# A transformer block on one core: the second MLP product as three passes over rounded parts, the keys' parts made in SBUF

## The reference, cut to what matters

```python
x_norm = modulate(_ln(x), shift_a, scale_a)
q, k, v = jnp.split(x_norm @ W_qkv + b_qkv, 3, axis=-1)
...                                   # softmax attention, W_proj, gate_a, residual
q_c = _ln(x) @ W_qc + b_qc
k_c, v_c = jnp.split(_ln(context) @ W_kvc + b_kvc, 2, axis=-1)
...                                   # softmax attention, W_cproj, residual
x_norm2 = modulate(_ln(x), shift_m, scale_m)
h = jax.nn.gelu(x_norm2 @ W_mlp1 + b_mlp1)
h = h @ W_mlp2 + b_mlp2               # the second MLP product
x = x + gate_m[:, None] * h
```

## Time and profile before

| | |
|---|---|
| median of 3 runs | 854.02 us (851.39 to 857.76) |
| profiled execution | 854.26 us, its span 852.4 us |
| PE busy | 814.3 us (96%) |
| DVE busy | 626.7 us (74%) |
| ACT busy | 489.6 us (57%) |
| POOL busy | 395.0 us (46%) |
| mean granted clock | 0.970 of full speed |

### The profile page before, as it was taken

How to read it: one execution, slowest core, us unless ns; L and a number is a source line. 1 busy time by engine, 2 the same in 40 slices (tenths; PEclk the granted TensorE clock), 3 DMA queues, 4 the chain that set the end, 5 groups by cost and what they waited for, 6 DMA issues and landing times.

```text
span 852.4 us, 19187 instructions
## 1 busy us (share of the span) xinstructions
PE 814.3 (96%) x6968; PEld 615.5 (72%) x6968; DVE 626.7 (74%) x1368; ACT 489.6 (57%) x923; POOL 395.0 (46%) x451
## 2 busy tenths in 40 slices
PE   6797989999999999999999999999999999998997
PEld 4666667778777777778787777777777778675776
DVE  5758897787868687887868787887868687764421
ACT  2153656657565656657575656657575656675242
POOL 3365446355454636365463637365463635251301
PEclk9698899999999999999999999999999999999899
DMA  7534453433434333433344343334334333211001
GB/s 261 163 115 137 143 157 114 110 114 111 129 114 134 108 122 118 126 96 119 120 114 137 105 129 117 119 95 126 112 114 142 100 104 107 65 39 62 26 1 38
DMA packets 92903, 95.05 MB, mean 112 GB/s; under 512 B 17993, under 2 KB 79562, under 8 KB 92426
## 3 DMA queue, kind: packets, MB, share of 16 engines
q1 hardware_dynamic: 91946, 92.77, 35.1%
q10 hardware_dynamic: 864, 1.07, 0.4%
HBM read 38.55 MB, written 4.32 MB: 50 GB/s over the span
## 4 chain that ended last, share of the span: by engine, by line
PE 88%; DVE 5%; POOL 2%; issue 2%; DMA 1%; ACT 1%; SPq 1%; DVEq 0%; ACTq 0%; POOLq 0%
PE bank L830 23%; PE scan L932 15%; PE pv L877 14%; PE bank L864 13%; PE bank L855 7%; PE bank L844 6%; PE score L942 5%; PE bank L804 2%; DVE MX_x L1297 1%; DMA P<-in_wm 1%; DVE MX_y L1297 1%; DVE W L1307 0%; ACT P L1092 0%; PE score L781 0%; DVE PT L1204 0%
## 5 line engine op out<-in xcount | busy, mean ns | idle before, releaser
L1092 ACT ACTIVATE P<-score 128x512 f32<-128x512 f32 x512 | 283.3, 598 | 217.9 <-PE score L942 215.9
L1297 DVE TENSOR_REDUCE MX_x<-scan 128x2 fp32r<-128x512 f32 x256 | 170.0, 678 | 66.5 <-PE scan L932 66.2
L1297 DVE TENSOR_REDUCE MX_y<-scan 128x2 fp32r<-128x512 f32 x256 | 165.3, 677 | 30.3 <-PE scan L932 28.9
L830 PE MATMUL bank<-xT_y,W 128*128 128x256 f32 x960 | 131.0, 293 | 5.2 <-DVE xT_y L1172 2.6
L830 PEld LDWEIGHTS bank<-xT_y,W 128*128 128x128 f32 x960 | 122.8, 198 | 10.8 <-issue 7.2
L864 PE MATMUL bank<-w_down,HH 128*128 128x256 f32 x512 | 125.6, 390 | 0.0
L932 PE MATMUL scan<-KS_x,QS_x 63*128 63x256 f32 x512 | 109.5, 324 | 8.4 <-DVE MX_x L1297 7.6
L932 PEld LDWEIGHTS scan<-KS_x,QS_x 63*128 63x128 f32 x512 | 72.4, 191 | 47.8 <-issue 22.8
L942 PE MATMUL score<-QS_y,KS_y 64*128 64x256 f32 x512 | 104.1, 318 | 1.4 <-ACT P L1092 1.4
L864 PEld LDWEIGHTS bank<-w_down,HH 128*128 128x128 f32 x512 | 93.0, 191 | 16.7 <-issue 0.6
L932 PEld LDWEIGHTS scan<-KS_y,QS_y 63*128 63x128 f32 x512 | 69.0, 190 | 48.9 <-DVE MX_y L1297 23.6
(11 more groups left out here) (139 smaller groups left out, 1272.2 us busy)
## 6 DMA issues: line engine op xcount, KB each, us to landing
KS_x<-SK SPq DMA_DIRECT2D x96, 128.0 KB, 2.1
KS_y<-SK SPq DMA_DIRECT2D x96, 128.0 KB, 2.1
...
```

Source lines behind the costliest of these rows:

```text
L830: last = nc.tensor.matmul(to[:, i * N:(i + 1) * N], w[p][:, c, (blk + i) * 128:(blk + i + 1) * 128], xT[k][:, q, c, :], start=(n == 0), st ...
L1092: nc.scalar.activation(P[:, s % 8, :, :].rearrange("p a n -> p (a n)"), score_bank[s % 2][:, :], ACT.Exp, scale=SCALE).then_inc(s_exp, 1)
L1297: nc.vector.tensor_reduce(MX[s1][:, half, col:col + NB], scan_bank[n % NSCAN][:, :].rearrange("p (a n) -> p a n", a=NB), AXIS.X, ALU.max, ...
```

## The change

1. **Second MLP product.** `w_down` becomes a part of `W`, split by a new task `w6` (HI on ACT, LO on DVE, 2048 columns each) in section B of t = 1, from `raw_down`, which now lies where LO will be. The gelu output goes to `hidden`, which lies over the LO half of a doubled `HH`; a new POOL task `h0` to `h3` casts 128x512 into HI and subtracts into LO (`rest`); for the last element DVE does that (`hidden_parts`). A half of `down` is now 4 x 3 = 12 `f32r` matmuls.
2. **Keys.** ACT writes `keys` (over the LO half of `SK`) from PSUM and then copies it to HI; POOL makes LO by a subtraction (`keys_rest`). The bank is free once `keys` is written. DVE's two instructions per key task go.
3. **Scratch** for dynamic transfers is set to 512 bytes, which makes room for the larger `HH` and `W`.
4. **The tables** are written anew for the steady sections; those of the first and last turns keep their order but for the added tasks.

```diff
-        w_down = sb("w_down", [128, FB, H])
+        w_down = weight(5120, FB, H)
...
+        keys = over("keys", [128, 2, N], sk_at + 4 * 2 * N)
...
+        HH, hh_at = placed("HH", [128, 2, FB, N], f32r)
+        hidden = over("hidden", [128, FB, N], hh_at + 4 * FB * N)
...
+            def keys_rest(name, b):
+                if name == "k_x" and b == 0:
+                    return
+                pool.wait_ge(s_hi[name], nth(name, b))
+                nc.gpsimd.tensor_tensor(SK[:, LO, :, :], keys[:, :, :], SK[:, HI, :, :].bitcast(fp32),
+                                        ALU.subtract).then_inc(s_lo[name], 1)
+
+            def rest(u, b):
+                if b == B - 1:
+                    return
+                pool.wait_ge(s_gelu[u], b + 1)
+                at = slice(2 * u, 2 * u + 2)
+                nc.gpsimd.tensor_copy(HH[:, HI, at, :], hidden[:, at, :]).then_inc(s_HH[u], 1)
+                pool.wait_ge(s_HH[u], 2 * b + 1)
+                nc.gpsimd.tensor_tensor(HH[:, LO, at, :], hidden[:, at, :], HH[:, HI, at, :].bitcast(fp32),
+                                        ALU.subtract).then_inc(s_HH[u], 1)
...
             def down(a, b, part, to):
                 if b == 0:
-                    pe.wait_ge(s_wdown, 16)
-                pe.wait_ge(s_HH, FB // 2 * b + FB // 4 * (part + 1))
+                    pe.wait_ge(s_wlo[6], 1)
+                for u in (2 * part, 2 * part + 1):
+                    pe.wait_ge(s_HH[u], 2 * b + 2)
                 for c in range(part * FB // 2, (part + 1) * FB // 2):
-                    last = nc.tensor.matmul(to[:, 0:H], HH[:, c, a * 128:(a + 1) * 128], w_down[:, c, :],
-                                            start=(c == 0), stop=(c == FB - 1))
+                    for n, (p, q) in enumerate(PARTS):
+                        last = nc.tensor.matmul(to[:, 0:H], HH[:, p, c, a * 128:(a + 1) * 128], w_down[q][:, c, :],
+                                                start=(c == 0 and n == 0), stop=(c == FB - 1 and n == 2))
...
                 for i in range(2):
-                    last = nc.scalar.activation(dst[:, HI, i, :], src[:, i * N:(i + 1) * N], ACT.Identity,
+                    to = keys[:, i, :] if name in ("k_x", "k_y") else dst[:, HI, i, :]
+                    last = nc.scalar.activation(to, src[:, i * N:(i + 1) * N], ACT.Identity,
                                                 bias=bias_cols[:, col + i:col + i + 1])
+                if name in ("k_x", "k_y"):
+                    last.then_inc(s_keys[name], 1)
+                    act.wait_ge(s_keys[name], nth(name, b))
+                    last = nc.scalar.activation(SK[:, HI, :, :].rearrange("p c n -> p (c n)"),
+                                                keys[:, :, :].rearrange("p c n -> p (c n)"), ACT.Copy)
...
+    "B1": [("q_x", 1, 4), ("q_x", -1, 6), ("k_y", 0, 15), ("w6", -1, 15)],
```

More of the change, by code:

```diff
@@ L28 @@
 SP_PLAN = {
[L29 to L32 removed]
+    "A": [("gate_a", 0, 0), ("xT_in", 2, 0), ("x_in", 2, 0), ("max_x0", 0, 1), ("st_c", 0, 3), ("q_y0", -1, 3),
+          ("mr_c", 0, 3), ("q_y1", -1, 6), ("k_x", 1, 7), ("max_x1", 0, 7), ("c_in", 1, 8), ("q_x", 1, 9), ("st_x",
+          2, 9), ("max_y0", -1, 10), ("mr_x", 2, 11), ("k_y", 0, 12), ("gate_m", -2, 14), ("cT_in", 1, 15)],
     "A-1": [("c_in", 1, 7), ("cT_in", 1, 12)],
@@ L93 @@
 ACT_PLAN = {
-    "A": [("v_x", 0, 1), ("up0", -3, 3), ("up1", -3, 3), ("T_x", 1, 3), ("up2", -3, 3), ("up3", -3, 3), ("T_y", -1,
-          8), ("k_x", 1, 8), ("q_y", -1, 10), ("q_x", 1, 13)],
+    "A": [("v_x", 0, 1), ("T_x", 1, 2), ("up0", -3, 3), ("up1", -3, 3), ("up2", -3, 3), ("up3", -3, 3), ("T_y", -1,
+          8), ("k_x", 1, 8), ("q_y", -1, 10), ("q_x", 1, 12)],
     "A-1": [],
@@ L106 @@
     "AB+2": [],
-    "B": [("v_y", -1, 3), ("k_y", 0, 9), ("T_m", -2, 11)],
+    "B": [("v_y", -1, 4), ("k_y", 0, 9), ("T_m", -2, 11)],
     "B0": [("q_x", 1, 8)],
-    "B1": [("q_x", 1, 4), ("q_x", -1, 6), ("k_y", 0, 15)],
+    "B1": [("q_x", 1, 4), ("q_x", -1, 6), ("k_y", 0, 15), ("w6", -1, 15)],
     "BB-1": [("T_m", -2, 12)],
@@ L237, in dram, with placed, over @@
             return nc.dram_tensor(name, shape, dt, kind="Internal").ap()
-        W = sb("W", [128, 2, 5120], f32r)
+        def placed(name, shape, dt):
+            at = (nc.sbuf_base + 31) // 32 * 32
+            return sb(name, shape, dt), at
+        def over(name, shape, at):
+            return nc.alloc_sbuf_tensor_at(name, shape, fp32, offset=at)
+        W, w_at = placed("W", [128, 2, 7168], f32r)
         def weight(start, blocks, cols):
@@ L307, in build @@
         raw_kvc = [to[:, :, :].rearrange("p a c -> p (a c)") for to in (x2, x2_bias)]
-        raw_up = HH[:, :, :].rearrange("p a b -> p (a b)")
-        rows = HH[0:B, 0:5, :]
+        raw_up, raw_down = [over(n, [128, 2048], w_at + 4 * (7168 + start))[:, :]
+                            for n, start in (("raw_up", 3072), ("raw_down", 5120))]
+        rows = hidden[0:B, 0:5, :]
         d_gate = dram("d_gate", (B, 4 * H))
@@ L355, in build @@
         s_centred = {k: sem(f"s_centred_{k}") for k in "xc"}
+        s_keys = {k: sem(f"s_keys_{k}") for k in ("k_x", "k_y")}
         s_hi = {k: sem(f"s_hi_{k}") for k in ("T_y", "q_x", "k_x", "q_y", "k_y")}
@@ L362, in build @@
         s_MT = {s: [sem(f"s_MT_{s}{i}") for i in range(2)] for s in "xy"}
-        s_HH = sem("s_HH")
+        s_gelu, s_HH = [[sem(f"{n}{u}") for u in range(4)] for n in ("s_gelu", "s_HH")]
         s_scan_full, s_scan_done = sem("s_scan_full"), sem("s_scan_done")
@@ L573, in load_down @@
             def load_down(b):
-                sp.dma_start(w_down[:, :, :], wdown).then_inc(s_wdown, 16)
+                sp.dma_start(raw_down, wdown).then_inc(s_raw[6], 16)
             def last_row_x0(b):
@@ L751, in _ @@
                 "sum0": lambda b: total(0, b), "sum1": lambda b: total(1, b),
+                **{f"h{u}": lambda b, u=u: rest(u, b) for u in range(4)},
+                **{k: lambda b, k=k: keys_rest(k, b) for k in ("k_x", "k_y")},
                 **{f"clear{i}": lambda b, i=i: clear(i) for i in range(5)}, "clear_V": clear_values,
@@ L979, in copied @@
             def copied(name, k, b):
-                wait(act, s_HH, FB // 2 * (b - 1))
+                for u in range(4):
+                    wait(act, s_gelu[u], b - 1)
                 src = full(act, name, b)
@@ L1078, in _ @@
                 "v_y": lambda b: values("y", b),
-                **{f"w{i}": lambda b, i=i: split_weight(i) for i in range(1, 6)},
+                **{f"w{i}": lambda b, i=i: split_weight(i) for i in range(1, 7)},
             }
@@ L1187, in projected @@
             def projected(name, dst, col, b):
-                if b == 0 and name in ("q_x", "k_x"):
-                    if name == "k_x":
-                        first_projected()
+                if b == 0 and name == "q_x":
                     return
@@ L1274, in _ @@
                 "q_y": lambda b: projected("q_y", SQ["y"], QYC, b),
-                "k_y": lambda b: projected("k_y", SK, KYC, b),
                 "q_x": lambda b: projected("q_x", SQ["x"], QXC, b),
-                "k_x": lambda b: projected("k_x", SK, KXC, b),
+                "k_x": first_projected,
+                **{f"h{u}": lambda b, u=u: hidden_parts(u, b) for u in range(4)},
                 "down0": lambda b: down(0, b),
                 "down1": lambda b: down(1, b),
-                **{f"w{i}": lambda b, i=i: split_weight(i) for i in range(1, 6)},
+                **{f"w{i}": lambda b, i=i: split_weight(i) for i in range(1, 7)},
                 "norm_x": norm_early, "T_x": lambda b: split_end("x", b),
```

101 lines of the change are left out of this document (58 added, 43 removed), and 29 rows, old and new, of tables (DVE_PLAN, PE_PLAN, POOL_PLAN).

## The result

| | before | after |
|---|---|---|
| median of 19 runs | 853.15 us (850.42 to 857.76) | 857.29 us (851.92 to 863.58) |
| ratio | | 1.0043, 95% interval 1.0025 to 1.0061 |
| profiled execution, span | 852.4 us | 855.8 us |
| mean granted clock | 0.970 | 0.952 |

A forecast was written before the change was run, and what follows sets the result against it. PE, busy 96% of the span, was taken to bound the steady turns. Terms -17.5 + 8.2 + 6.3 + 1.5 + 1.3 + 0.2 = 0.0 against the profiled 854.26 us gave 854 us, range 842 to 866.

The forecast's parts named there:

- the halves: Second product on PE: 57 halves at 0.29 us less each, plus 1.0 for the last four, -17.5 us.
- contention in the steady turns: Steady turns: POOL's later `norm_x` delays the gelu table load, leaving PE's fourth `up` quarter 0.2 us spare; +1.3 (0 to 6).
- start-up, the keys: Start-up: element 1's `k_x` takes 0.6 on ACT and 1.3 on POOL instead of DVE's two instructions; +0.2 us.
- w6 with the clock: Uncovered split of `w_down` delays first maxima of t = 2, +8.2 (5 to 10); slower clock after it, +1.5.
- the end: t = 15 and 16: `root_y` behind POOL's pairs, +2.6 and +2.2, keys ahead of `T_m`, +1.5; 6.3 (4 to 9).
- What bounds the kernel: PE bounds the steady turns, shortened to about 46.5 us; POOL rises to about 35 us without becoming the bound.
- what PE saves: Each half of the second product takes 1.70 instead of 1.99 us on PE; -17.5 us in all.
- the one new wait as long or longer is w6's: PE's clock drops only after the wait for the `w_down` split; +1.5 (0 to 4, if `T_y`'s waits also lower it).
- My own sign of being wrong: PE reaching section B of t = 2 less than 5 or more than 10 us later than before.
- The keys' subtraction ahead of `T_m`: At t = 16 `k_y` of element 15 precedes `T_m` of element 13 on POOL, delaying PE's first `up`; +1.5 us.
- The rival of POOL's lateness: Steady turns: `norm_x` 0.2 us late delays the gelus; about 1 us per turn, +12, 866 us; chance 0.17.

The follow-up runs named there:

- Experiment 3: Changed kernel with POOL doing `root_y` ahead of the last pair `h3` at t = 15 and 16; ratio to before 0.9982, median 6.4 us below the changed kernel's.
- experiments 9 and 8: 9: changed kernel with element 15's `k_y` as before, ratio to before 1.0047; 8: that plus `gate`, `w6`, t=2 tables, element 1's `k_x` and `root_y` re-placed, 0.9848.
- experiment 4: Changed kernel with only element 1's `k_x` made as before (HI by ACT, LO by DVE, both from PSUM); ratio to before 1.0044.

## Why the prediction was near and not right

The measured terms come from the segments above. A half is worth a quarter of the difference of one steady turn, section A of t = 8 to that of t = 9, (47.73 - 46.44) / 4 = 0.3225 us; 4 halves lie in A of 2 to A of 4, 44 in A of 4 to A of 15, and of those behind I count 9, with 7.07 - 5.81 = 1.26 for the last four. The halves are 57 x 0.3225 + 1.26; each other term is its segment's difference with the halves in it added back: -13.4 + 14.2, +3.5, 6.6 + 1.3, and 6.7 + 2.9 + 1.3. So "contention" is only what is left over, and all of them rest on one execution each.

| term | predicted | measured |
|---|---|---|
| the halves | -17.5 | -19.6 |
| contention in the steady turns | +1.3 | +0.8 |
| start-up, the keys | +0.2 | +3.5 |
| w6 with the clock | +9.7 | +7.9 |
| the end | +6.3 | +10.9 |
| sum | 0.0 | +3.5 |

- **What bounds the kernel** and **what PE saves** were right: PE is busy throughout, a turn is 46.43 (46.5 forecast), POOL at 34.75 (about 35). The half was taken as 1.70 from a row of the first product; it takes 1.64.
- **The end** is the step that failed: +6.3, and 10.9 measured. Its waits came as worked out: `root_y` ended 3.3 later against PE's other work, exactly the term, and PE waited 2.55 and 1.96 (2.6 and 2.2 forecast). But I wrote that "the one new wait as long or longer is w6's", and gave the clock to that alone. It fell behind both waits for `T_y` as well (0.61 in 730 to 734, 0.58 in 778 to 782). Experiment 3 shows the price: 4.5 us of waits taken away gave 6.8, where the terms had 4.8. I had that in the range only. What else is missing to 10.9 lies by the profiles at `k_y` of element 15 (3.4 and 4.1 us by experiments 9 and 8, +1.5 forecast), which the medians don't confirm. The Trainium skill, page "TensorE: Matmul & The Clock Gate", section "HAM oscillation — how this bites in real kernels", has the mechanism, that the engine restarts slow after starving; the trace agrees, and the fault was to apply it once.
- **Start-up** is the second term that was off: +0.2, and 3.5 in this pair of executions. The copy was priced by its 0.6 us. Whether it is the clock (0.57 for 1.00) that turns it into some 3 is not settled: by experiment 4 the same code has anything from 0.50 to 0.81 there.
- **w6**: the place is right, and the size nearly (DVE's split 2.63 in place of 3.59). My own sign of being wrong did come: PE reached B of t = 2 11.1 us later than before (132.1 to 121.0), over my 10; 3.5 of it were there already at A of t = 2. That its wait has no cover was right of `w6`, but I overlooked that `w_gated`, moved on POOL behind `norm_x`, waits at the same point. Undoing `w6` alone therefore gained only 3.4 us, and by that price I would have named a wrong cause.
- **The keys' subtraction ahead of `T_m`** at t = 16: PE's 0.95 us are there; what they cost in time is open, as said.
- **The rival of POOL's lateness** did not come true, and its place was wrong: `norm_x` did no harm, the deadline near by is the second quarter's LO part, 1.6 us off. I had said that 0.2 us of lateness decide; that a deadline was in fact close by was luck, since I had worked it out for another task. My later belief in 11 us of slack, read from POOL's idle time, was the worse reading.
- **The near hit** is in part luck too: the halves and `w6` came out 3.9 us better than forecast, start-up and the end 7.9 worse.
